# Radial weights ahead of the second transposed block in the first edge pass of a graph kernel

## The chip, the cores and the metric

One core of a Trainium2 chip runs the whole program. The metric is the device time of one execution in microseconds. The chip has a matrix engine (TensorE, PE in the rows), a vector engine (VectorE, DVE), an activation engine (ScalarE, ACT), a general engine that here only issues gathers (GpSimd, POOL) and an engine that issues DMAs (SyncE, SP). Each works through its own instructions in order; they meet at semaphores.

## The reference

Two message-passing layers over a graph with 12,500 nodes and 200,000 edges, each with a residual and a layer norm. The change concerns the edges of the first layer. For each edge, with `y0, y1` from `edge_attr_4` and weights `w1` from `edge_attr_16`:

```python
msg_s = (s_n @ Ws_src)[src] + (s_n @ Ws_dst)[dst]          # 64 scalars
msg_v = (v_n x Wv_src)[src] + (v_n x Wv_dst)[dst]          # 32 vectors of 3
w1 = rbf @ W_rbf                                           # radial weights, 224 an edge
m1_s, m1_v = _cg_tp(msg_s, msg_v, y0, y1, *parts of w1)    # first product
a = leaky(m1_s @ W_alpha) . alpha_dot                      # logits of 4 heads
val_s = m1_s @ Ws_val;  val_v = (m1_v x Wv_val) * sigmoid(val_s @ Wg)
m2_s, m2_v = _cg_tp(sigmoid(val_s), val_v, y0, y1, w2...)  # second product
h = concat(m2_s @ Ws_vlin, m2_v x Wv_vlin)                 # values of 4 heads
```

A softmax over each node's edges, the weighted sum, a projection and the second layer follow in later passes.

## The kernel before

The kernel runs its passes one after the other; the first edge pass is the function `edges`. It takes the edges in 392 groups of 512, a group being 4 tiles of 128 edges. An edge is a partition (row) for VectorE's products; TensorE needs channels in the partitions, so each product is transposed by TensorE into PSUM (`ps_t`, two banks in turn), and ScalarE copies each bank out (`take`), after which TensorE multiplies by weights.

The order of work is written out by hand, an instruction list for each engine in a `body(u, ...)` that a loop repeats four groups at a time (`rounds`). Everything waits on counting semaphores: `first` counts VectorE's steps of the first product (14 a group), `turned` TensorE's blocks, `taken` ScalarE's copies, `radial` and `weighted` the radial weights made and scaled, `second`, `third`, `mixed`, `gated`, `headed`, `kept`, `valued` later steps. The loops are staggered: while group u has its first product transposed, the radial weights of u + 1 are made, the second product of u - 1 is under way, and the values of u - 2.

Steps that matter here, with their names in the profile:
- VectorE: `message` adds the two gathered rows (e_msg). `products_with_y` multiplies them by scaled harmonics that stand beside the radial weights in PSUM (e_vy and e_c, L1013), so it waits for `weighted`. Sums and cross products follow, then `heads_with_y` (e_partial), `scalars_by_weights`, `heads_sum` (e_h, L1014), `vectors_by_weights` and `cross_by_weights`; with the last of these `first` reaches 14. In one group of four `leaky` (logits) follows and waits for ScalarE's `keep`. The next group's messages alternate with the gating of the group before.
- TensorE: `radial_weights(u + 1)` is four bf16 matmuls (L784) into `ps_w`, a single buffer: it waits until VectorE has finished group u. `scalars`, `vectors`, `last_block` are four transposes each (L793), of the first, second and third block of the first product. `vectors` waits for the same count of `first` as `radial_weights`. `first_layer` (L809) waits for the second `take`; `values(u - 2)` (L849, L850), `mix(u)` (L818 to L820, waits for the third `take`), `second_blocks(u - 1)` (L793) and `heads(u - 1)` (L838, waits for VectorE's e_h) follow in this order.
- ScalarE: `harmonics` issues the DMA that loads `y` of group u + 1 (L916), `store` one of results; then three times `take` (L886), `with_y0` (L963 once and L966 four times: copies the harmonics beside the radial weights and scales the weights by y0 in place; waits for `radial` and the load of `y`), the hidden layer (L901, L902), `second_with_y0` (L941), the gate and logits (L905 to L907, waits for `mixed`), two takes of the second product (e_m2t), and `keep` (e_above L926, e_partial L928, waits for `headed`).
- GpSimd issues the gathers three groups ahead; SyncE loads indices and radial bases.

Of the kernel before, what the change touches and what calls it, by code (L numbers as in the profile page):

```python
# [35 lines left out]
RING = 4  # L36
# [32 lines left out]
def wait(engine, sem, value):  # L69

    if not isinstance(value, int) or value > 0:
        engine.wait_ge(sem, value)
# [466 lines left out]
def edges(nc, walk, idx_d, y_d, rbf_d, table_src, table_dst, h_d, w, ident, logits, issued, dst_windows, dst_i, windows_in):  # L539
# [13 lines left out]
    with ExitStack() as ctx:  # L553
# [99 lines left out]
        def turn(u, second_tp, k):  # L653


            if second_tp:
                return u * 6 + ((5 if isinstance(u, int) and u == groups - 1 else 9) + k)
            return k + 1 if isinstance(u, int) and u == 0 else u * 6 + (k - 1)
# [13 lines left out]
        def present(u):  # L672

            return not isinstance(u, int) or 0 <= u < groups
# [94 lines left out]
        def _(pe):  # L769
# [10 lines left out]
            def radial_weights(u, r, i):  # L780
                pe.wait_ge(rbf_in[r], (i + 1) * 16 * len(PARTS_OF_PAIRS))
                wait(pe, first, u * FIRST)
                for t in range(T):
                    last = nc.tensor.matmul(radial_w[:, t, 0:WN],  # L784
                                            rbf[:, r, t * P:(t + 1) * P], stack_rbf[:], start=True, stop=True)
                last.then_inc(radial, 1)

            def turn_block(place, bank, rows):

                wait(pe, taken, place - 2)  # L790
                for t in range(T):
                    channels = rows(t).shape[1]
                    last = nc.tensor.transpose(ps_t[bank][0:channels, t * P:(t + 1) * P], rows(t), ident[:])  # L793
                last.then_inc(turned, 1)

            def scalars(u):
                pe.wait_ge(first, u * FIRST + DONE_S)
                turn_block(turn(u, False, 0), 0, lambda t: m1[:, t, 0:MID])

            def vectors(u):  # L800
                pe.wait_ge(first, (u + 1) * FIRST)
                turn_block(turn(u, False, 1), 1, lambda t: m1[:, t, MID:MID + P])

            def last_block(u):
                turn_block(turn(u, False, 2), 0, lambda t: m1[:, t, MID + P:MID + 2 * P])

            def first_layer(u):
                pe.wait_ge(taken, turn(u, False, 1))
                nc.tensor.matmul(ps_t[1][:], w_first[:], m1t[0:MID, 0, :], start=True, stop=True).then_inc(turned, 1)  # L809
# [43 lines left out]

            def body(u, r, i):
                scalars(u)
                vectors(u)
                if present(u + 1):
                    radial_weights(u + 1, (r + 1) % RING, i + (r + 1) // RING)
                last_block(u)
                first_layer(u)  # L860
                values(u - 2)
                mix(u)
                second_blocks(u - 1)
                heads(u - 1, (r - 1) % 2)

            radial_weights(0, 0, 0)
            rounds(pe, body)
            values(groups - 2)
            second_blocks(groups - 1)
# [3 lines left out]
        @block.scalar  # L873
        def _(act):
            act.wait_ge(ones_set, 1)

            def rotations(r):

                vector = y[:, r, :, 1:4]
                lanes, tiles, components = vector.ap  # L880
                return bass.AP(vector.tensor, vector.offset, [lanes, tiles, [components[0], 3], components])

            def take(place, bank, into):
                act.wait_ge(turned, place)
                rows = into.shape[0]
                nc.scalar.activation(into, ps_t[bank][0:rows, :], ACT.Copy).then_inc(taken, 1)  # L886

            def body(u, r, i):
                slot = r % 2
                wait(act, mixed, u)  # L890
                if present(u + 1):
                    harmonics(u + 1, (r + 1) % RING)
                store(u - 3, 1 - slot)
                take(turn(u, False, 0), 0, m1t[0:MID, 0, :])
                take(turn(u, False, 1), 1, m1t[:, 1, :])
                take(turn(u, False, 2), 0, m1t[:, 2, :])
                with_y0(u + 1, (r + 1) % RING, i + (r + 1) // RING)
                act.wait_ge(turned, turn(u, False, 3))
                wait(act, headed, u - 1)

                nc.scalar.activation(hidden[0:CS, slot, :], ps_t[1][0:CS, :], ACT.Relu, scale=0.8)  # L901
                nc.scalar.activation(hidden[CS:P, slot, :], ps_t[1][CS:P, :], ACT.Sigmoid).then_inc(taken, 1)  # L902
                second_with_y0(u - 1, (r - 1) % RING)
                act.wait_ge(mixed, u + 1)
                nc.scalar.activation(gate, gate, ACT.Sigmoid)  # L905
                nc.scalar.activation(second_y, rotations(r), ACT.Copy)
                nc.scalar.activation(logits[:, bass.ds(u * T, T), :], mix_v[:, :, LIN:LIN + HEADS],  # L907
                                     ACT.Copy).then_inc(gated, 1)
                take_second(u - 1)
                keep(u - 1, (r - 1) % RING, 1 - slot, i)  # L910

            def harmonics(u, r):

                if present(u - RING):
                    act.wait_ge(third, (u - RING + 1) * THIRD)
                act.dma_start(y[:, r], y_d[u]).then_inc(y_in[r], 16)  # L916

            def keep(v, r, slot, i):
                if not present(v):
                    return  # L920
                act.wait_ge(headed, v + 1)
                if present(v - 2):
                    act.wait_ge(third, (v - 1) * THIRD)
                if r == 0:
                    wait(act, leaked, i)
                nc.scalar.activation(above[:, r], mix_h[:, :, HL:HL + HEADS], ACT.Copy)  # L926
                for t in range(T):
                    last = nc.scalar.activation(partial[:, slot, t, HS:HA], mix_h[:, t, HS:HA], ACT.Copy,  # L928
                                                scale=y[:, r, t, 0:1])
                last.then_inc(kept, 1)  # L930

            def second_with_y0(v, r):

                if not present(v):
                    return
                act.wait_ge(second, v * SECOND + GV)
                if present(v - 1):
                    act.wait_ge(turned, turn(v - 1, True, 1))
                for t in range(T):
                    into = m2[:, t, 0:6 * CV].rearrange("p (x k c) -> p x k c", x=3, k=2)  # L940
                    last = nc.scalar.activation(into[:, :, 0, :], gv[:, t], ACT.Copy, scale=y[:, r, t, 0:1])  # L941
                last.then_inc(scaled_v, 1)

            def take_second(v):
                if not present(v):
                    return
                wait(act, valued, v)
                take(turn(v, True, 0), 0, m2t[:, 0, :])
                take(turn(v, True, 1), 1, m2t[0:MID, 1, :])

            def store(v, slot):
                if not present(v):
                    return
                act.wait_ge(third, (v + 1) * THIRD)
                act.dma_start(h_d[v], h_rows[:, slot].rearrange("p t k -> p (t k)")).then_inc(stored[slot], 16)

            def with_y0(u, r, i):

                if not present(u):
                    return  # L960
                act.wait_ge(radial, u + 1)
                act.wait_ge(y_in[r], (i + 1) * 16)
                nc.scalar.activation(first_y, rotations(r), ACT.Copy)  # L963
                for t in range(T):
                    of_tile = radial_w[:, t, W_SS:W_SS + MID]
                    last = nc.scalar.activation(of_tile, of_tile, ACT.Copy, scale=y[:, r, t, 0:1])  # L966
                last.then_inc(weighted, 1)

            harmonics(0, 0)
            with_y0(0, 0, 0)  # L970
            rounds(act, body)
            second_with_y0(groups - 1, RING - 1)
            take_second(groups - 1)
            store(groups - 3, (groups - 3) % 2)
            keep(groups - 1, RING - 1, (groups - 1) % 2, 0)
            store(groups - 2, groups % 2)
            store(groups - 1, (groups - 1) % 2)
            for slot in range(2):
                act.wait_ge(stored[slot], 16 * (groups // 2))
# [1573 lines left out]
```

## Time and profile before

| | us |
|---|---|
| median of 3 runs | 9161.6 |
| lowest, highest | 9114.37, 9190.41 |
| the profiled execution | 9135.79 |
| its span in the profile | 9134.0 |
| first radial matmul of the pass, start | 242.9 |
| last radial matmul of the pass, start | 5470.6 |

The profile shows one execution. Its span runs from the first to the last instruction; the execution's own time is 1.8 us longer. The first edge pass fills the span from about 243 to about 5,500 us. Ends of matmuls are modelled, not observed. In the timeline, instructions of one kind in a row are merged (x4), with the time from the start of the first to the end of the last, and the bracket at the end is the time that the engine was idle before and what ended it.

### The profile page before, as it was taken

What the parts mean: (1) busy time and instruction counts of PE and PEld (TensorE: products, weight loads), DVE (VectorE), ACT (ScalarE), POOL (GpSimd) and SP (SyncE); (2) the same over time, 40 slices, a digit from 0 to 9 for tenths busy, and PEclk for the clock granted to TensorE, in tenths of its full rate; (3) what the DMA queues carried; (4) which work ended last, traced back from release to release, by engine and by line L of the source; (5) the groups of instructions that cost most, each with busy time, mean ns of one, the idle gap of its engine ahead of it and who ended that gap; (6) DMA issues with size and microseconds to landing.
All of it is one profiled execution on the core that took longest, in us unless ns stands there. A gap on an engine that the chain in (4) does not pass through costs nothing. (4 is left out here: it accounts for less than half of the span.)

```text
span 9134.0 us, 197714 instructions
## 1 busy us (share of the span) xinstructions
PE 7569.2 (83%) x43972; PEld 5972.6 (65%) x43973; DVE 6766.6 (74%) x16742; ACT 5161.1 (57%) x16950; POOL 5109.3 (56%) x5222
## 2 busy tenths in 40 slices
PE   5788888888888888888888886997778888888788
PEld 3677777777777777777777776995444444444446
DVE  7777777777777777777777787887667767767677
ACT  5555555555555555555555552116666666667675
POOL 0556666555555555655655555870666655566650
PEclk7788888888788788888888797998899989999999
DMA  7333333223222232322332234766444434444345
GB/s 251 79 83 87 85 85 84 79 83 85 79 83 83 79 85 83 84 83 81 84 83 83 82 80 150 236 204 112 107 110 111 112 106 110 111 109 114 108 110 180
DMA packets 971877, 968.06 MB, mean 106 GB/s; under 512 B 452750, under 2 KB 788750, under 8 KB 971662
## 3 DMA queue, kind: packets, MB, share of 16 engines
q0 software_dynamic: 225792, 385.65, 17.1%
q1 hardware_dynamic: 512032, 346.40, 13.8%
q10 hardware_dynamic: 233936, 234.90, 7.7%
q14 instruction: 98, 0.80, 0.0%
q8 instruction: 19, 0.31, 0.0%
HBM read 677.57 MB, written 288.65 MB: 106 GB/s over the span
## 5 line engine op out<-in xcount | busy, mean ns | idle before, releaser
L754 POOL DMA_INDIRECT e_g_dst<-table_dst,e_idx x1568 | 1518.9, 969 | 1159.5 <-issue 622.8
L754 POOL DMA_INDIRECT e_g_src<-table_src,e_idx x1568 | 1560.9, 995 | 996.6 <-issue 803.3
L2028 POOL DMA_INDIRECT f_e<-table,f_src x1568 | 1494.0, 953 | 980.1 <-issue 530.3
L793 PE MATMUL e_ps_t<-ident,e_m 128*128 128x128 f32 (+1 forms) x7840 | 1405.9, 331 | 471.1 <-issue 193.2
L793 PEld LDWEIGHTS e_ps_t<-ident,e_m 128*128 128x128 f32 (+1 forms) x7840 | 1121.6, 168 | 618.4 <-issue 365.8
L2085 PE MATMUL f_ps_a<-sums 128*128 128x384 f32 x3936 | 1524.3, 534 | 1.5 <-DVE sums L2185 1.5
L2085 PEld LDWEIGHTS f_ps_a<-sums 128*128 128x128 f32 x3936 | 767.6, 205 | 576.0 <-issue 228.7
L886 ACT ACTIVATE e_m1t<-e_ps_t 128x512 f32<-128x512 f32 (+1 forms) x1176 | 669.1, 597 | 548.9 <-PE e_ps_t L809 198.1
L2074 PE MATMUL f_ps_w<-f_w,f_hidden 64*128 64x192 f32 x3936 | 495.1, 374 | 470.3 <-DVE sums L2185 232.3
L1013 DVE TENSOR_TENSOR e_vy<-e_msg,e_ps_w 128x384 f32<-128x384 f32 x392 | 216.5, 552 | 839.5 <-issue 522.1
L905 ACT ACTIVATE e_ps_v<-e_ps_v 128x128 f32<-128x128 f32 x392 | 102.7, 262 | 1252.7 <-remote 733.3
L838 PE MATMUL e_ps_h<-e_w_hs,e_hidden 128*128 128x100 f32 x3136 | 582.1, 345 | 257.3 <-DVE e_h L1014 195.4
L838 PEld LDWEIGHTS e_ps_h<-e_w_hs,e_hidden 128*128 128x128 f32 x3136 | 516.1, 249 | 357.7 <-DVE e_h L1014 281.9
L849 PEld LDWEIGHTS e_ps_h<-e_w_h,e_m2t 128*128 128x128 f32 x3136 | 562.7, 211 | 229.1 <-issue 217.6
L819 PE MATMUL e_ps_v<-e_w_v,e_m1t 128*128 128x64 f32 x3136 | 709.4, 311 | 1.5 <-issue 1.4
L850 PE MATMUL e_ps_h<-e_w_h,e_m2t 96*128 96x96 f32 x3136 | 705.1, 310 | 0.0
L2074 PEld LDWEIGHTS f_ps_w<-f_w,f_hidden 64*128 64x128 f32 x3936 | 337.1, 201 | 554.7 <-DVE sums L2185 279.1
L2185 DVE TENSOR_TENSOR f_ey<-f_e,f_ps_w 128x384 f32<-128x384 f32 x492 | 272.5, 554 | 558.6 <-ACT f_ps_w L2118 264.3
L820 PE MATMUL e_ps_v<-e_w_v,e_m1t 128*128 128x64 f32 x3136 | 666.4, 297 | 2.5 <-DVE e_m L1015 1.2
L2130 ACT ACTIVATE sums<-iota,f_rel 128x128 f32<-128x128 f32 x1968 | 628.6, 390 | 16.0
L818 PE MATMUL e_ps_v<-e_w_gate,e_m1t 96*128 96x36 f32 x3136 | 615.1, 282 | 24.8 <-DVE e_d L1013 11.8
L849 PE MATMUL e_ps_h<-e_w_h,e_m2t 128*128 128x64 f32 x3136 | 598.7, 275 | 2.4 <-ACT e_partial L928 2.4
(268 smaller groups left out, 17539.2 us busy)
## 6 DMA issues: line engine op xcount, KB each, us to landing
edge_values<-e_h ACTq DMA_DIRECT2D x392, 330.0 KB
r_h<-edge_values SPq DMA_DIRECT2D x196, 660.0 KB, 4.0
sums<-sums ACTq DMA_DIRECT2D x492, 192.0 KB
e_g_src<-table_src,e_idx POOLq DMA_INDIRECT x1568
e_g_dst<-table_dst,e_idx POOLq DMA_INDIRECT x1568
f_e<-table,f_src POOLq DMA_INDIRECT x1568
f_rbf<-basis SPq DMA_DIRECT2D x492, 48.0 KB
basis<-t_part SPq DMA_DIRECT2D x42, 448.0 KB, 3.1
```

Source lines behind the costliest of these rows:

```text
L754: pool.indirect_dma_start(out=into[:, r, t, :], out_offset=None, in_=table, in_offset=bass.IndirectOffsetOnAxis(ap=idx[:, r, c:c + 1], axi ...
L793: last = nc.tensor.transpose(ps_t[bank][0:channels, t * P:(t + 1) * P], rows(t), ident[:])
L819: nc.tensor.matmul(mix_v[:, t, VS:VS + 2 * CV], m1t[:, 1, tile], w_v1[:], start=True, stop=True)
L820: last = nc.tensor.matmul(mix_v[:, t, VS + 2 * CV:VS + 4 * CV], m1t[:, 2, tile], w_v2[:], start=True, stop=True)
L838: last = nc.tensor.matmul(mix_h[:, t, HS:HL + HEADS], hidden[:, slot, t * P:(t + 1) * P], w_hs[:], start=True, stop=True)
L849: nc.tensor.matmul(mix_h[:, t, 0:2 * CV], m2t[:, 0, tile], w_h1[:], start=True, stop=True)
L850: last = nc.tensor.matmul(mix_h[:, t, 2 * CV:HA], m2t[0:MID, 1, tile], w_h2[:], start=True, stop=True)
L886: nc.scalar.activation(into, ps_t[bank][0:rows, :], ACT.Copy).then_inc(taken, 1)
L2028: pool.indirect_dma_start(out=rows_of_units[:, (place * RING + r) * T + t, :], out_offset=None, in_=table, in_offset=bass.IndirectOffsetOn ...
L2074: last = nc.tensor.matmul(ps_w[r % 2][:, t * 256:t * 256 + WE], hidden[rows, r % 2, n * P:(n + 1) * P], w_2[rows, :], start=True, stop=True)
L2085: last = nc.tensor.matmul(ps_a[slot][:, 0:ACC1], onehot[:, r, t, :], q[:, r, t, :], start=t == 0, stop=t == T - 1)
L2130: last = nc.scalar.activation(apart[:, r % 2, t, :], iota[:], ACT.Abs, bias=rel[:, r % 2, t:t + 1])
```

## The change

TensorE's list makes the radial weights of group u + 1 after the first block of transposes, ahead of the second one. ScalarE's list scales them after the first `take`, ahead of the second and third one. Nothing else differs: the instructions, buffers, tiles and other waits are the same.

```diff
--- before.py
+++ after.py
@@ -853,9 +853,9 @@
 
             def body(u, r, i):
                 scalars(u)
-                vectors(u)
                 if present(u + 1):
                     radial_weights(u + 1, (r + 1) % RING, i + (r + 1) // RING)
+                vectors(u)
                 last_block(u)
                 first_layer(u)
                 values(u - 2)
@@ -892,9 +892,9 @@
                     harmonics(u + 1, (r + 1) % RING)
                 store(u - 3, 1 - slot)
                 take(turn(u, False, 0), 0, m1t[0:MID, 0, :])
+                with_y0(u + 1, (r + 1) % RING, i + (r + 1) // RING)
                 take(turn(u, False, 1), 1, m1t[:, 1, :])
                 take(turn(u, False, 2), 0, m1t[:, 2, :])
-                with_y0(u + 1, (r + 1) % RING, i + (r + 1) // RING)
                 act.wait_ge(turned, turn(u, False, 3))
                 wait(act, headed, u - 1)
```

## Rows read from the trace of the kernel before

**Rows 1.** Page, part 1: busy time, share of the span and instructions of each engine.

```profile
PE 7569.2 (83%) x43972; PEld 5972.6 (65%) x43973; DVE 6766.6 (74%) x16742; ACT 5161.1 (57%) x16950; POOL 5109.3 (56%) x5222
```

**Rows 2.** Busy time by engine in 500:5400, then granted clock, DMA share, GB/s.

```profile
500.00:5400.00 4900.00, 4169.29 (x26992) 3668.71 (x26991) 3672.54 (x9216) 2718.94 (x8753) 2884.76 (x2939) 0.83 0.31 83
```

**Rows 3.** Groups by line, 500:5400: count | busy, mean ns | idle before, releasers.

```profile
L838 PE MATMUL e_ps_h<-e_w_hs,e_hidden 128*128 128x100 f32 x2913 | 540.1, 344 | 241.2 <-DVE e_h L1014 180.9 <-issue 53.3
...
L809 PE MATMUL e_ps_t<-e_m1t,e_w_first 96*128 96x512 f32 x730 | 462.3, 719 | 28.0 <-ACT e_m1t L886 15.1 <-issue 12.6
...
L784 PE MATMUL e_ps_w<-e_stack_rbf,e_rbf 96*128 96x224 bf16 x1457 | 248.7, 303 | 0.0
...
L1013 DVE TENSOR_TENSOR e_vy<-e_msg,e_ps_w 128x384 f32<-128x384 f32 x365 | 201.6, 552 | 799.3 <-issue 498.5 <-ACT e_ps_w L966 300.8
...
L905 ACT ACTIVATE e_ps_v<-e_ps_v 128x128 f32<-128x128 f32 x365 | 95.6, 262 | 1189.2 <-remote 706.4 <-PE e_ps_v L820 443.9 <-issue 38.6
...
L926 ACT ACTIVATE e_above<-e_ps_h 128x16 f32<-128x16 f32 x364 | 67.1, 184 | 287.2 <-PE e_ps_h L838 230.4 <-issue 29.8 <-remote 26.8
...
L1014 DVE TENSOR_TENSOR logits<-logits,e_above 128x64 f32 x91 | 20.6, 226 | 241.2 <-ACT e_partial L928 153.1 <-issue 88.1
```

**Rows 4.** Timeline, ScalarE, one group: start, duration, instruction, idle before.

```profile
3195.07 0.18 ACT L926 ACTIVATE e_above<-e_ps_h 128x16 f32<-128x16 f32 x1 [1.07 <-PE e_ps_h L838]
...
3195.29 0.34 ACTq L916 DMA_DIRECT2D e_y<-harmonics  x1
...
3196.27 1.08 ACT L886 ACTIVATE e_m1t<-e_ps_t 96x512 f32<-96x512 f32 x2 [0.19 <-PE e_ps_t L793]
3198.69 0.60 ACT L886 ACTIVATE e_m1t<-e_ps_t 128x512 f32<-128x512 f32 x1 [1.34 <-PE e_ps_t L809]
3199.18 0.20 ACT L963 ACTIVATE e_ps_w<-e_y 128x36 f32<-128x36 f32 x1
3199.30 1.00 ACT L966 ACTIVATE e_ps_w<-e_ps_w,e_y 128x96 f32<-128x96 f32 x4
...
3205.87 0.26 ACT L905 ACTIVATE e_ps_v<-e_ps_v 128x128 f32<-128x128 f32 x1 [3.27 <-remote]
...
3206.23 1.07 ACT L886 ACTIVATE e_m2t<-e_ps_t 128x512 f32<-128x512 f32 x2
3207.84 0.18 ACT L926 ACTIVATE e_above<-e_ps_h 128x16 f32<-128x16 f32 x1 [0.54 <-PE e_ps_h L838]
```

**Rows 5.** Timeline of VectorE, the same group.

```profile
3200.43 0.56 DVE L1013 TENSOR_TENSOR e_vy<-e_msg,e_ps_w 128x384 f32<-128x384 f32 x1 [4.60 <-issue]
...
3203.65 0.55 DVE L1013 TENSOR_TENSOR e_partial<-e_ps_h,e_y 128x384 f32<-128x384 f32 x1
...
3204.91 0.81 DVE L1014 TENSOR_TENSOR e_h<-e_partial,e_ps_h 128x640 f32<-128x640 f32 x1
```

**Rows 6.** Timeline of TensorE, the same group.

```profile
3194.83 1.21 PE L793 MATMUL e_ps_t<-ident,e_m 128*96 128x128 f32 x8
3195.88 0.55 PE L784 MATMUL e_ps_w<-e_stack_rbf,e_rbf 96*128 96x224 bf16 x4
3196.92 0.66 PE L793 MATMUL e_ps_t<-ident,e_m 128*128 128x128 f32 x4 [0.49 <-issue]
3197.41 1.12 PE L809 MATMUL e_ps_t<-e_m1t,e_w_first 96*128 96x512 f32 x2
...
3199.87 0.41 PE L850 MATMUL e_ps_h<-e_w_h,e_m2t 96*128 96x96 f32 x2
...
3202.55 0.39 PE L820 MATMUL e_ps_v<-e_w_v,e_m1t 128*128 128x64 f32 x2
...
3205.77 2.03 PE L838 MATMUL e_ps_h<-e_w_hs,e_hidden 128*128 128x100 f32 x8 [1.02 <-issue]
```

**Rows 7.** DMA issues of the whole run: count, KB, us to landing.

```profile
t_wb<-w_Wv_src SPq DMA_DIRECT2D x4, 4.0 KB, 1.7
...
m_wp_b<-w_Wpv SPq DMA_DIRECT2D x4, 4.0 KB, 4.9
```

## The prediction

> **What bounds the kernel now.** I began with the page's busy shares: TensorE 83%, VectorE 74%, ScalarE 57% of the span [rows 1], so no engine is full and the change must be judged by waits. The edited stage is the first edge pass. The window 500:5400 lies inside it, with TensorE busy 4169.29 of 4900 us and VectorE 3672.54, at a granted clock of 0.83 [rows 2]. Grouping by line in that window gives 365 groups (one "e_vy<-e_msg" each) [rows 3], so a group of 512 edges takes 4900/365 = 13.42 us, and the pass has 392 of them.
>
> Next I asked the same rows for the idle time ahead of each instruction. VectorE loses nearly all it loses in one place: 799.3 us, 2.19 us a group, ahead of the first product with the scaled radial weights, ended mostly by "issue" and by ScalarE's L966, the instruction that scales them [rows 3]. That is what the change aims at. But three other waits recur too: TensorE 241.2 us ahead of the heads matmuls (0.66 a group, mostly for VectorE's e_h), ScalarE 287.2 us ahead of e_above (0.79 a group, for those matmuls), and ScalarE 1189.2 us ahead of the gate (3.26 a group) [rows 3].
>
> Then I walked one typical group (12.77 us from one e_above to the next) on the three engines. ScalarE: e_above 3195.07; the first two takes 3196.27 to 3197.35; the third 3198.69; radial scaling 3199.18 to 3200.30; the gate only at 3205.87; the second product's takes until 3207.30; next e_above 3207.84 [rows 4]. VectorE: first product 3200.43, e_h 3204.91 to 3205.72 [rows 5]. TensorE: first and second transposes 3194.83 to 3196.04, radial weights 3195.88, third transposes 3196.92, first layer 3197.41, last of the mixing matmuls 3202.55, heads 3205.77 to 3207.80 [rows 6]. So there are **two loops through the same e_above**:
> - Loop A: first take, (second and third take), radial scaling, VectorE's products to e_h, heads, e_above. It closes the group here: heads start 0.05 us after e_h ends.
> - Loop B: first and second take, first layer, value and mixing matmuls, gate, two takes of the second product, e_above. Here it ends at 3207.30, only 0.54 us ahead of loop A.
> The reader is to see how close they are: A is shortened by the change and B is lengthened.
>
> **The change part by part.** No instruction is added or removed. On TensorE four radial matmuls pass four transposes; on ScalarE five activations pass two takes. Both waits that move along are met: the radial matmuls wait for the same count of VectorE as the second transposes did, and TensorE was idle 0.0 us ahead of the radial matmuls in the window, so their inputs were always there [rows 3].
>
> 1. *Radial weights earlier.* They took 3195.88 to 3196.43 and now start where the second transposes did, halfway through the eight at about 3195.43, so they are done by about 3196.0, ahead of the end of the first take at 3196.27 + 0.60 = 3196.87 (0.60 as the third one took) [rows 4, 6]. No cost. The second transposes come 0.55 us later, end by 3196.6 instead of about 3196.05, and their take is not ready to begin before 3197.9 now, so that is covered too. If TensorE's signals come late (below), the cover is gone and ScalarE's whole queue waits behind the scaling; bounds 0 and about 1 us.
>
> 2. *Scaling earlier.* It starts at about 3196.8 instead of 3199.18, 2.4 us earlier; VectorE can use 2.19 a group on average, its idle time. Not all: in one group of four VectorE waits 241.2/91 = 2.65 us for ScalarE's e_partial ahead of the logits sum [rows 3], and this wait stands ahead of its messages and gating, which come before the next product, so in these groups the product gains nothing. What the group gains is bounded by what waits for VectorE at the other end: 0.66 us (TensorE ahead of heads) to 0.79 us (ScalarE ahead of e_above). In the group walked, loop B takes over after 0.54. I take a gain of 0.5; bounds 0 and 0.79.
>
> 3. *The harmonics' transfer.* The scaling reads what ScalarE's queue issued at 3195.29 [rows 4]. That was 3.9 us before its use, now 1.5. Its landing isn't shown; the nearest rows are 4 KB loads at 1.7 us and, farther, 4.9 us in a busier stage [rows 7]. So 0.1 to 3.4 us of wait; I take 0.1, by the row of 1.7 us.
> The Trainium skill (DMA: Bandwidth & Descriptors, Anatomy of one DMA) gives a fixed cost of about 2.0 us whatever the size; by it the wait would be 0.5 us, 0.4 more a group and some 150 us in all. The 1.7 us row here is under that figure.
>
> 4. *Second and third take later.* The scaling lasts 1.12 us (3199.18 to 3200.30) and now lies ahead of the second take, which ends at about 3198.45 instead of 3197.35. Queued behind it are the third take and, on TensorE, the first layer, which waits for the second take; behind that in TensorE's order are the value matmuls, the mixing, the second transposes and the heads. First layer: 3197.41 becomes 3198.5, +1.1 us. The granted clock of 0.83 on average [rows 2] says that TensorE spends a third of the time at the lower of its two levels (1.2 against 2.4 GHz); there its transposes last longer and the first layer comes later anyway, so the mean is less; bounds 0.4 and 1.1, I take 1.0. The third take is not delayed: it waited for TensorE until 3198.69 and now ends near 3199.05.
>
> 5. *How much of that 1.0 us reaches the gate.* The last mixing matmul is shown ending at 3202.94, yet ScalarE's gate, with nothing else to wait for, starts at 3205.87 [rows 4, 6]; over all groups such waits, ended by "remote", make 706.4/365 = 1.94 us [rows 3]. TensorE's signals are up to 3 us behind its shown ends. If this is backlog that a pause works off, a pause of 1 us ahead of the first layer costs less than 1 us; if it is a delay after each burst, the pause costs all of itself. No row tells which; bounds 0 and 1.0 given back, I take 0.4.
> The Trainium skill (Perfetto Trace Analysis, Tensor Engine Instruction) says that the profiler estimates a matmul's end and that the semaphore follows only after PSUM's acknowledgement. The trace agrees that the shown end is no signal, with 2.93 us between the two here.
>
> Per group: -0.5 (step 2) + 0.1 (step 3) + 1.0 (step 4) - 0.4 (step 5) = +0.2 us. Times 392: +78 us. The profiled execution took 9135.8 us (span 9134.0), 26 under the median of the three runs (9161.6) and inside their range. 9135.8 + 78 = 9214, rounded to **9215 us**.
>
> **The rivals.**
> - *Loop A's gain comes through*: the pause is absorbed in the late signals. For it: VectorE's 2.19 us a group, and heads released by e_h within 0.05 us. Against: only 0.66 to 0.79 us can come back. Net -0.3 to -0.5 a group: 9018 to 8940 us.
> - *Loop B takes the place of A at its full new length* (the other side): the second take stands behind the scaling, the first layer starts 1.0 us later, and the delay reaches the gate whole. It decides as soon as more than the 0.5 us of slack arrives. Net -0.4 + 1.0 + 0.1 = +0.7: 9410 us. For it: loop B was 0.54 us behind, and TensorE at 4169.29 of 4900 has little to catch up with. At the lower clock level its work is longer and its slack smaller still.
> - *VectorE's gain stops halfway*: after the cross products it reads the value matmuls' result. It read it at 3203.65 [rows 5] and would come at about 3201.3, while these matmuls, shown ending at 3200.28 before [rows 6], now end at 3201.4 plus the late signal. It then waits 0.1 to 3 us of the 2.4. e_h is still earlier than now in most groups, so this costs nothing alone; it takes step 2 towards 0. With that: +0.7 as above.
>
> **How the numbers follow.** About 1%, some 92 us or 0.23 us a group, is what the measurement can tell from no change. Forecast case (within 0.23 of zero either way, likeliest value +0.2): 0.38. Loop A's gain: 0.27, faster by over 1%. Loop B in full, with its variants between +0.23 and +0.8: 0.35, slower by over 1%. The range takes most of the first rival (-0.32 x 392 = -125) and most of the second (+0.68 x 392 = +265): 9010 to 9400 us.
>
> **What the changed profile would show.** VectorE's idle time ahead of "e_vy<-e_msg" under 0.8 us a group (right for steps 1 and 2); TensorE's wait for e_h ahead of heads nearly gone; a new wait ahead of the first layer (L809) of about 1 us a group for ScalarE's takes (step 4); VectorE waiting ahead of "e_partial<-e_ps_h" for the value matmuls. A wait of the scaling for harmonics over 0.3 us would prove step 3 wrong. Step 5 shows in the "remote" idle time ahead of the gate: below 1.94 us a group means that the pause is absorbed. The prediction fails towards faster if that falls by 1 us, towards slower if it stays.

## The result, and the profile after

| | us |
|---|---|
| before, median of 3 runs | 9161.6 (9114.37 to 9190.41) |
| changed, median of 3 runs | 9564.66 (9563.63 to 9600.56) |
| ratio | 1.046, 95% interval 1.042 to 1.0501 |
| changed, the profiled execution | 9600.56 (span 9598.8) |

The changed kernel is 4.6% slower, 403 us by the medians. Nearly all of the loss is in the first edge pass: its last radial matmul starts at 5921.8 us, against 5470.7 before, which is 451 of the 465 us by which the two spans differ.

The page, parts 1 and 2 (the second line is the granted clock of TensorE in 40 slices of the span, in tenths). TensorE is busy for 288 us more than before with the same 43972 instructions [rows 1]: the work has become longer, not more.

```profile
PE 7856.8 (82%) x43972; PEld 6286.7 (65%) x43973; DVE 6785.1 (71%) x16742; ACT 5214.9 (54%) x16950; POOL 5131.4 (53%) x5222
...
PEclk7777777778778787888887887899899999999999
```

Two more lines of the kernel before, in the window 500:5400: count | busy, mean ns of one | idle before, with releasers.

```profile
L819 PE MATMUL e_ps_v<-e_w_v,e_m1t 128*128 128x64 f32 x2920 | 662.1, 312 | 1.5 <-issue 1.4
...
L1013 DVE TENSOR_TENSOR e_partial<-e_ps_h,e_y 128x384 f32<-128x384 f32 x365 | 200.1, 548 | 44.4 <-remote 31.8 <-PE e_ps_h L850 10.8 <-issue 1.2
```

The changed kernel in the same window:

```profile
L819 PE MATMUL e_ps_v<-e_w_v,e_m1t 128*128 128x64 f32 x2688 | 704.7, 353 | 0.0
...
L809 PE MATMUL e_ps_t<-e_m1t,e_w_first 96*128 96x512 f32 x672 | 462.7, 776 | 423.0 <-ACT e_m1t L886 230.4 <-issue 192.4
L838 PE MATMUL e_ps_h<-e_w_hs,e_hidden 128*128 128x100 f32 x2683 | 459.1, 329 | 36.5 <-DVE e_h L1014 28.3 <-issue 7.9
...
L1013 DVE TENSOR_TENSOR e_partial<-e_ps_h,e_y 128x384 f32<-128x384 f32 x336 | 186.6, 555 | 324.6 <-PE e_ps_h L850 230.6 <-issue 58.7 <-remote 31.4
...
L1013 DVE TENSOR_TENSOR e_vy<-e_msg,e_ps_w 128x384 f32<-128x384 f32 x336 | 184.6, 549 | 417.0 <-issue 285.9 <-ACT e_ps_w L966 130.6
...
L905 ACT ACTIVATE e_ps_v<-e_ps_v 128x128 f32<-128x128 f32 x335 | 87.8, 262 | 1400.1 <-PE e_ps_v L820 1130.4 <-remote 222.2 <-issue 47.4
L963 ACT ACTIVATE e_ps_w<-e_y 128x36 f32<-128x36 f32 x336 | 69.8, 208 | 107.0 <-DMA e_y<-harmonics 47.0 <-remote 27.5 <-issue 24.9
...
L926 ACT ACTIVATE e_above<-e_ps_h 128x16 f32<-128x16 f32 x336 | 62.0, 185 | 205.4 <-PE e_ps_h L838 187.7 <-remote 17.2 <-issue 0.6
```

And the busy time of the window by engine (TensorE, its weight loads, VectorE, ScalarE, GpSimd), then granted clock, DMA share, GB/s.

```profile
500.00:5400.00 4900.00, 4072.55 (x24859) 3635.48 (x24857) 3394.41 (x8483) 2551.43 (x8061) 2659.30 (x2693) 0.79 0.28 76
```

There are 336 groups in 4900 us, so a group takes 14.58 us instead of 13.42. Against [rows 3], per group:
- VectorE waits 417.0/336 = 1.24 us ahead of e_vy (before 2.19) and now also 324.6/336 = 0.97 us ahead of e_partial, for the value matmuls (before 44.4/365 = 0.12).
- TensorE waits 36.5/336 = 0.11 us for e_h ahead of the heads (before 0.66). Loop A has let go.
- TensorE waits 423.0/336 = 1.26 us ahead of the first layer, for ScalarE's takes (before 28.0/365 = 0.08). This is the new wait.
- ScalarE's "remote" idle time ahead of the gate is 222.2/335 = 0.66 us (before 1.94).
- ScalarE waits 107.0/336 = 0.32 us ahead of the scaling, of which 47.0/336 = 0.14 us for the load of the harmonics.
- The same mixing matmul (L819) takes 353 ns on average, before 312. This is what the prediction has no term for. The granted clock of the window is 0.79, before 0.83 [rows 2].

Two groups of the changed kernel, only one group between them, show what a mean hides. Stretches by window, same columns; the first is a whole group, the second another whole group, the third and fourth two parts that make up nearly all of that second one.

```profile
3716.10:3727.69 11.59, 9.59 (x76) 8.38 (x75) 10.37 (x28) 7.61 (x24) 6.91 (x7) 1.00 0.32 89
...
3739.80:3757.47 17.67, 14.51 (x66) 13.09 (x65) 10.59 (x28) 7.75 (x24) 9.18 (x10) 0.61 0.24 68
3739.80:3743.40 3.60, 0.77 (x6) 0.42 (x4) 1.47 (x4) 2.96 (x12) 2.62 (x3) 1.00 0.61 176
3743.40:3757.20 13.80, 13.47 (x58) 12.40 (x59) 8.85 (x24) 4.78 (x13) 6.29 (x8) 0.51 0.14 37
```

One group lasts 11.59 us at a clock of 1.00, the other 17.67 us. In the first 3.6 us of the long one TensorE is busy for 0.77 us, at full clock still; then the granted clock falls to the lower level, and the 13.8 us behind it hold 13.47 us of matmuls. TensorE's timeline in the short group (start, duration, instruction, idle before):

```profile
3717.94 0.66 PE L793 MATMUL e_ps_t<-ident,e_m 128*128 128x128 f32 x4 [0.50 <-issue]
3719.89 1.12 PE L809 MATMUL e_ps_t<-e_m1t,e_w_first 96*128 96x512 f32 x2 [1.29 <-ACT e_m1t L886]
...
3722.61 0.34 PE L818 MATMUL e_ps_v<-e_w_gate,e_m1t 96*128 96x36 f32 x2
...
3724.79 0.41 PE L819 MATMUL e_ps_v<-e_w_v,e_m1t 128*128 128x64 f32 x2
...
3725.26 1.04 PE L793 MATMUL e_ps_t<-ident,e_m 128*128 128x128 f32 x8
```

and in the long one:

```profile
3741.67 0.66 PE L793 MATMUL e_ps_t<-ident,e_m 128*128 128x128 f32 x4 [1.76 <-issue]
3743.73 2.08 PE L809 MATMUL e_ps_t<-e_m1t,e_w_first 96*128 96x512 f32 x2 [1.40 <-issue]
...
3748.96 0.53 PE L818 MATMUL e_ps_v<-e_w_gate,e_m1t 96*128 96x36 f32 x2
...
3753.14 0.67 PE L819 MATMUL e_ps_v<-e_w_v,e_m1t 128*128 128x64 f32 x2
...
3754.02 1.92 PE L793 MATMUL e_ps_t<-ident,e_m 128*128 128x128 f32 x8
```

TensorE idles for 1.76 us ahead of the third transposes (0.50 in the short group). They are over at 3742.33, the first layer starts at 3743.73 after another 1.40 us without a matmul, and then lasts 2.08 us instead of 1.12; the mixing takes 5.3 us (3748.96 to 3754.23) instead of 2.8 (3722.61 to 3725.4). ScalarE's timeline in the long group tells why TensorE paused: the scaling lies between the first take and the two others, and the gate then waits out the slow matmuls.

```profile
3741.03 0.59 ACT L886 ACTIVATE e_m1t<-e_ps_t 96x512 f32<-96x512 f32 x1 [0.22 <-issue]
...
3742.17 0.99 ACT L966 ACTIVATE e_ps_w<-e_ps_w,e_y 128x96 f32<-128x96 f32 x4
3743.06 1.10 ACT L886 ACTIVATE e_m1t<-e_ps_t 128x512 f32<-128x512 f32 x2
...
3754.27 0.26 ACT L905 ACTIVATE e_ps_v<-e_ps_v 128x128 f32<-128x128 f32 x1 [6.04 <-PE e_ps_v L820]
```

I took groups 20 to 379 from the records of both kernels, from one e_above to the next, and sorted them by the share of each that fell under the lower level (1.2 GHz) of the granted clock:

| share at the low level | before: groups, mean us | after: groups, mean us |
|---|---|---|
| under 1% | 66, 12.36 | 142, 12.41 |
| 1% to 65% | 245, 13.03 | 98, 13.69 |
| over 65% | 49, 16.84 | 120, 17.67 |
| all | 360, 13.43 | 360, 14.51 |

**At the high level the change costs and brings nothing; most of the loss is in where the low level falls.** From the start of the first layer to the gate, a group spent 1.97 us at the low level before and 4.03 us after; in the rest of the group that time fell from 2.57 to 1.93 us. A straight line, fitted in each kernel to the lengths of the groups with these two times, starts at 12.32 us in both. With the low-level times of before, the line of the changed kernel gives 13.61 us, so by this estimate some 0.9 of the added 1.1 us come from the low level's new place and 0.2 from the rest. As a mean over the groups, 16% of the stretch of the mixing and 15% of that of the values lay at the low level before, 43% and 40% after; for the first block of transposes it fell from 46% to 24%. Before, TensorE's long pause lay ahead of the heads, and the heads and the short transposes behind it bore much of the slow stretch; now a longer one lies ahead of its longest unbroken work.

The Trainium skill (TensorE: Matmul & The Clock Gate, A second HAM failure mode: psum-queue depth-cycling) tells of another kernel that short, frequent idle times of TensorE between groups of matmuls made its clock swing between the two levels. The traces here agree that it swings, with a mean grant of 0.83 before and of 0.79 with 1.26 us of pause a group ahead of the first layer.

### The profile page after: what moved, and what is told of

Read it like the earlier page. It is cut to its first block and busy times, and to the rows that moved or that the text cites. A ratio compares the mean times of both kernels' runs of the same rounds, so it can differ in the third digit from the quotient of the medians.

```text
span 9598.8 us, 197330 instructions
## 1 busy us (share of the span) xinstructions
PE 7856.8 (82%) x43972; PEld 6286.7 (65%) x43973; DVE 6785.1 (71%) x16742; ACT 5214.9 (54%) x16950; POOL 5131.4 (53%) x5222
## 5 line engine op out<-in xcount | busy, mean ns | idle before, releaser
L793 PE MATMUL e_ps_t<-ident,e_m 128*128 128x128 f32 (+1 forms) x7840 | 1364.0, 315 | 417.5 <-issue 211.6
L793 PEld LDWEIGHTS e_ps_t<-ident,e_m 128*128 128x128 f32 (+1 forms) x7840 | 1064.0, 162 | 545.0 <-issue 279.5
L809 PE MATMUL e_ps_t<-e_m1t,e_w_first 96*128 96x512 f32 x784 | 537.8, 774 | 489.5 <-ACT e_m1t L886 256.2
L819 PE MATMUL e_ps_v<-e_w_v,e_m1t 128*128 128x64 f32 x3136 | 821.3, 353 | 0.0
L850 PE MATMUL e_ps_h<-e_w_h,e_m2t 96*128 96x96 f32 x3136 | 817.8, 351 | 0.0
L849 PEld LDWEIGHTS e_ps_h<-e_w_h,e_m2t 128*128 128x128 f32 x3136 | 652.8, 244 | 248.1 <-issue 210.8
L820 PE MATMUL e_ps_v<-e_w_v,e_m1t 128*128 128x64 f32 x3136 | 774.5, 338 | 0.0
L818 PE MATMUL e_ps_v<-e_w_gate,e_m1t 96*128 96x36 f32 x3136 | 706.6, 315 | 0.3 <-issue 0.3
L849 PE MATMUL e_ps_h<-e_w_h,e_m2t 128*128 128x64 f32 x3136 | 681.7, 307 | 2.4 <-ACT e_partial L928 2.4
L818 PEld LDWEIGHTS e_ps_v<-e_w_gate,e_m1t 96*128 96x128 f32 x3136 | 640.5, 253 | 1.6 <-issue 1.6
L820 PEld LDWEIGHTS e_ps_v<-e_w_v,e_m1t 128*128 128x128 f32 x3136 | 640.8, 253 | 0.0
L819 PEld LDWEIGHTS e_ps_v<-e_w_v,e_m1t 128*128 128x128 f32 x3136 | 640.4, 252 | 0.0
```

Of the source, the lines that this page charges most:

```text
L818: nc.tensor.matmul(mix_v[:, t, 0:VS], m1t[0:MID, 0, tile], w_gate[:], start=True, stop=True)
L819: nc.tensor.matmul(mix_v[:, t, VS:VS + 2 * CV], m1t[:, 1, tile], w_v1[:], start=True, stop=True)
L820: last = nc.tensor.matmul(mix_v[:, t, VS + 2 * CV:VS + 4 * CV], m1t[:, 2, tile], w_v2[:], start=True, stop=True)
L849: nc.tensor.matmul(mix_h[:, t, 0:2 * CV], m2t[:, 0, tile], w_h1[:], start=True, stop=True)
L850: last = nc.tensor.matmul(mix_h[:, t, 2 * CV:HA], m2t[0:MID, 1, tile], w_h2[:], start=True, stop=True)
```

## The experiments

Ratios are each kernel's to the kernel before, measured beside it on the same chip. The kernel before took 9094.88 us beside e1 to e4 (chip 2), 9486.02 beside e5 to e8 and 9495.25 beside e9 to e12 (both chip 4), and 9085.69 beside e13 to e15 (chip 0). So times are compared on one chip only, and waits or mean durations of e5 to e12 stand beside those of a kernel before whose profiled execution took 9135.79 us.

**Theories.** *Queue*: the first layer's delay passes through to the gate. *Clock*: the pause ahead of the first layer brings the lower clock to the value and mixing matmuls. *Earlier VectorE work* (contention) and *TensorE's order* are further rivals.

**e1, the delay alone.** On the kernel before:

```diff
             def first_layer(u):
-                pe.wait_ge(taken, turn(u, False, 1))
+                pe.wait_ge(taken, turn(u, False, 2))
```

> The kernel before, with one wait changed: the first layer waits for ScalarE's third take instead of the second. Nothing of VectorE's work comes earlier, so this is the delay of the first layer alone. Before, the first layer starts about 2.7 us after e_above and the third take ends about 4.1 us after it, so the delay is some 1.4 us a group. If a delay there passes whole to the end of the group (theory of the queue), +0.9 to 1.3 us a group of 392, 9,500 to 9,650 us. If a delay alone is absorbed and only TensorE's clock costs (theory of the clock), the groups at the high clock level keep their length (12.4 to 12.9 us) and more groups run at the low one. If both are absorbed: under 9,250 us.

Measured 9750.53 us, ratio 1.0705 (1.0648 to 1.0762). Groups by line, 500:5400:

```profile
L819 PE MATMUL e_ps_v<-e_w_v,e_m1t 128*128 128x64 f32 x2616 | 713.1, 366 | 0.0
...
L809 PE MATMUL e_ps_t<-e_m1t,e_w_first 96*128 96x512 f32 x656 | 436.1, 751 | 463.7 <-ACT e_m1t L886 286.3 <-issue 177.4
```

The pause is 463.7/328 = 1.41 us a group and L819 takes 366 ns. By the records of groups 20 to 379 the first layer starts 1.3 us later than before. The groups with under 1% at the low level lasted 12.46 us, against 12.36 before; 112 instead of 49 had over 65%, and the low level took 4.66 us a group between first layer and gate, against 1.97. So a delayed first layer without any of the change's other effects makes more than the whole loss. Where the clock holds, the delay is absorbed; where it doesn't, it is not: these groups last 17.70 us, against 16.84.

**e2, e13, e14, e15, the pause filled with useless work.** On the changed kernel; e15 issues these transposes twice:

```diff
+            def fill(u):
+                for t in range(T):
+                    nc.tensor.transpose(ps_t[0][:, t * P:(t + 1) * P], m1[:, t, MID + P:MID + 2 * P], ident[:])
...
                 vectors(u)
+                pe.wait_ge(taken, turn(u, False, 0))
+                fill(u)
                 last_block(u)
```

> The changed kernel, with the third block's transposes made twice: four more transposes a group, in the stretch in which TensorE would only wait for the second take. The first layer still waits for that take, so the delay stays and only the pause is filled. Theory of the clock (the pause lets the granted clock fall for the value and mixing matmuls): fewer groups at the low level, about 9,200 to 9,400 us. Theory of the queue (the first layer's delay is passed on): as the changed kernel, 9,565 us, or up to 100 us more for the added work.

> The changed kernel again, unaltered, so that it and the filled ones stand against the same runs of the kernel before on one chip. Ratio 1.04 to 1.05, as in its own result.

> e2 again (four more transposes in the wait for the second take) on the chip of e13. Theory of the clock: 0.015 to 0.03 in the ratio under e13. If e2's lower ratio came from another chip, the two are equal, or this one is above e13.

> Eight more transposes a group instead of four, 1.1 us or more of work without use. The pause left in e2 ahead of the first layer (0.7 us a group) falls to about 0.3. Theory of the clock: the value and mixing matmuls run at the high level as often as in the kernel before or more (mean of L819's counterpart under 320 ns), ratio 1.00 to 1.025, limited by the added work where the clock is low. Theory of the queue: the ratio rises over e13's by the added work.

| | added | us | ratio | interval |
|---|---|---|---|---|
| e2 | 4 transposes | 9286.89 | 1.0224 | 1.0165 to 1.0283 |
| e13 | none | 9562.63 | 1.0535 | 1.0473 to 1.0596 |
| e14 | 4 transposes | 9266.31 | 1.0169 | 1.0097 to 1.0241 |
| e15 | 8 transposes | 9126.5 | 1.0032 | 1.0007 to 1.0057 |

Groups by line and the window, e13, e14 (L823 and L813 are its L819 and L809) and e15:

```profile
L819 PE MATMUL e_ps_v<-e_w_v,e_m1t 128*128 128x64 f32 x2672 | 706.0, 356 | 0.0
...
L809 PE MATMUL e_ps_t<-e_m1t,e_w_first 96*128 96x512 f32 x668 | 454.7, 768 | 438.0 <-ACT e_m1t L886 251.9 <-issue 185.7
```

```profile
500.00:5400.00 4900.00, 4068.36 (x24726) 3640.19 (x24725) 3377.37 (x8434) 2534.06 (x8017) 2643.51 (x2673) 0.79 0.29 76
```

```profile
L823 PE MATMUL e_ps_v<-e_w_v,e_m1t 128*128 128x64 f32 x2832 | 668.2, 323 | 0.0
...
L813 PE MATMUL e_ps_t<-e_m1t,e_w_first 96*128 96x512 f32 x709 | 472.3, 753 | 264.7 <-issue 154.8 <-ACT e_m1t L892 109.4
```

```profile
500.00:5400.00 4900.00, 4112.49 (x27620) 3653.53 (x27618) 3577.20 (x8946) 2671.47 (x8502) 2824.16 (x2842) 0.86 0.30 80
```

```profile
L823 PE MATMUL e_ps_v<-e_w_v,e_m1t 128*128 128x64 f32 x2912 | 652.4, 309 | 0.0
...
L813 PE MATMUL e_ps_t<-e_m1t,e_w_first 96*128 96x512 f32 x726 | 436.6, 685 | 113.2 <-issue 66.4 <-ACT e_m1t L892 44.4
```

```profile
500.00:5400.00 4900.00, 4197.03 (x29807) 3751.06 (x29807) 3668.88 (x9173) 2719.43 (x8717) 2905.77 (x2926) 0.90 0.31 83
```

The pause goes from 438.0/334 = 1.31 us a group to 0.75 to 0.31; the mixing matmul from 356 ns to 323 to 309; the granted clock from 0.79 to 0.86 to 0.90. The changed kernel gets **436 us faster by eight transposes a group that nobody reads**. By the theory of the queue it had to get slower, so that theory alone can't hold. By the records of groups 20 to 379 the first layer starts 3.81 us after e_above in e2 and in e15 and 3.80 in the changed kernel, so its lateness alone is not the price; the time at the low level between first layer and gate is 2.20 us a group in e2 and 1.28 in e15, against 4.03.

**e7, the same amount of work in the wrong place.** The last tile's three mixing matmuls are issued twice, in the changed kernel:

```diff
-                for t in range(T):
+                for t in (*range(T), T - 1):
                     tile = slice(t * P, (t + 1) * P)
                     nc.tensor.matmul(mix_v[:, t, 0:VS], ...
```

> Control for the filled pause: the changed kernel with as much added work (the last tile's three mixing matmuls issued twice, about 0.7 us a group), but in the dense stretch and not in the pause. Theory that the filled pause helped since it was filled: no gain here, 0.7 us x 392 = 270 us more, ratio 1.06 to 1.08. Theory that any added TensorE work holds the clock up: a ratio under 1.04.

Measured 10097.92 us, ratio 1.0643 (1.061 to 1.0676). The changed kernel wasn't measured on that chip, but e5, whose pause is the same and which loses as much, was at 1.0454. More work in this dense stretch costs; the same amount in the pause helped.

**e5 and e6, the halves of the change.** e5 moves only the scaling on ScalarE, e6 only the radial matmuls on TensorE; each is one hunk of the diff.

> Only ScalarE's half of the change: the scaling ahead of the second and third take, TensorE's order as before. The first layer waits for the second take behind the scaling just as in the changed kernel, and the radial weights come 0.6 us later. If the pause ahead of the first layer is the cause, the loss is the changed kernel's or larger: ratio to the kernel before 1.04 to 1.06.

> Only TensorE's half of the change: radial weights between the first and second transposes, ScalarE's order as before. The second take comes some 0.5 us later at most and no pause opens ahead of the first layer. Expected: within 1% of the kernel before (ratio 0.995 to 1.01). A ratio over 1.03 would say that TensorE's order, not ScalarE's, made the loss.

e5: 9900.8 us, 1.0454 (1.0424 to 1.0484), pause 425.5/327 = 1.30 us. e6: 9625.54 us, 1.0179 (1.0124 to 1.0234), pause 157.9/341 = 0.46 us, L819 328 ns. ScalarE's half alone makes a loss as large as the whole one. I had expected e6 within 1%. The second take ends 0.6 us later there, by the moved transposes, and opens a smaller pause; but the scaling, still behind all three takes, starts later too (4.30 us after e_above, before 3.97), and VectorE waits 906.8/341 = 2.66 us for it (before 2.19):

```profile
L1013 DVE TENSOR_TENSOR e_vy<-e_msg,e_ps_w 128x384 f32<-128x384 f32 x341 | 188.8, 554 | 906.8 <-ACT e_ps_w L966 481.3 <-issue 425.5
```

How e6's loss divides between the two is not shown.

**e3 and e12, useful work in the pause.**

```diff
                 last_block(u)
-                first_layer(u)
                 values(u - 2)
+                first_layer(u)
                 mix(u)
```

e3 does this to the changed kernel, e12 to the kernel before.

> The changed kernel, with the value matmuls of group u - 2 ahead of the first layer instead of behind it: 2 us of useful work fill the pause, and the mixing matmuls start about 1 us earlier than in the changed kernel. Both theories expect a gain over 9,565 us here. If the late first layer was all of the loss and loop A's gain is real, the time falls to 9,000 to 9,150 us, under the kernel before. If the hidden layer, now later by 2 us, holds ScalarE and the second product up, it stays at 9,300 us or above.

> The kernel before with the value matmuls ahead of the first layer and nothing else. It has hardly a pause ahead of the first layer (0.08 us a group), so the theory of the pause expects no gain: ratio 0.99 to 1.01. A ratio near 0.98 would say that e3's return to the level of before came from the value matmuls' place itself, not from the filled pause.

e3: 9111.29 us, 1.0001 (0.9975 to 1.0026). e12: 9519.91 us, 1.0045 (1.0017 to 1.0073). Groups by line of e3:

```profile
L819 PE MATMUL e_ps_v<-e_w_v,e_m1t 128*128 128x64 f32 x2912 | 686.5, 322 | 0.2 <-issue 0.2
...
L809 PE MATMUL e_ps_t<-e_m1t,e_w_first 96*128 96x512 f32 x728 | 441.6, 692 | 37.5 <-ACT e_m1t L886 19.6 <-issue 17.1
```

The pause is 0.10 us, L819 is back at 322 ns, and the loss is gone; e12 shows that the new place of the value matmuls brings nothing by itself. But I had hoped for less than the time before, and that isn't there, though ScalarE's wait ahead of the gate is down to 610.1/365 = 1.67 us and VectorE's ahead of e_vy to 396.8/364 = 1.09. What bounds e3 was not tried.

**e4, e9, e10, the scaling between the second and third take.** ScalarE's order is take, take, scaling, take. e9 leaves TensorE's order as before, e4 takes the changed one, e10 the changed one with the value matmuls first.

> TensorE's order as changed; ScalarE scales the radial weights between the second and the third take instead of between the first and the second. The first layer isn't delayed, the third take is (by 1.1 us, and the mixing matmuls reach it later than that). Scaling starts about 1.7 us earlier than before. Theory that the second take's delay behind the scaling is the cause of the loss: the loss is gone, and a part of the gain shows, 8,950 to 9,150 us. Theory that earlier VectorE work itself is the cause (contention, a lower clock from a denser TensorE): slower than before, 9,250 us or more.

> TensorE's order as before; ScalarE scales the radial weights between the second and the third take. Compared with the run e4, the second transposes are not moved behind the radial matmuls, so the second take isn't later and the first layer keeps its place: idle time ahead of it under 0.15 us a group (e4 had 0.26, the kernel before 0.08). Theory of the pause ahead of the first layer: no loss, ratio 0.985 to 1.00. Were e4's loss due to earlier VectorE work, it would stay: 1.01.

> e4 (scaling between second and third take, radial weights between first and second transposes) with the value matmuls ahead of the first layer. No pause ahead of the first layer in any case. Theory: ratio 0.98 to 1.00, at least 0.01 under e4's 1.012.

e4: 9202.79 us, 1.0116 (1.0065 to 1.0167), pause 92.8/358 = 0.26 us. e9: 9453.9 us, 0.9955 (0.992 to 0.9989). e10: 9492.62 us, 0.9969 (0.9948 to 0.9991). Groups by line of e9:

```profile
L838 PE MATMUL e_ps_h<-e_w_hs,e_hidden 128*128 128x100 f32 x2832 | 496.0, 330 | 158.6 <-DVE e_h L1014 95.9 <-issue 60.8
L809 PE MATMUL e_ps_t<-e_m1t,e_w_first 96*128 96x512 f32 x708 | 480.4, 767 | 34.0 <-issue 20.6 <-ACT e_m1t L886 12.8
...
L1013 DVE TENSOR_TENSOR e_vy<-e_msg,e_ps_w 128x384 f32<-128x384 f32 x354 | 195.0, 551 | 443.2 <-issue 255.1 <-ACT e_ps_w L966 188.1
```

e9 takes 0.94 us off VectorE's wait ahead of e_vy (443.2/354 = 1.25 us), keeps the pause at 34.0/354 = 0.10 us, and is 0.45% faster than the kernel before, a small gain with 1 just outside its interval. e4 was expected at or under the time before and is over it. It has TensorE's changed order and 0.26 us of pause, but they were not separated, and VectorE's wait for e_vy is 514.4/358 = 1.44 us there, so that the pause makes e4's loss is argued, not shown. e3 and e9 speak against earlier VectorE work as a cause of the loss: the scaling starts 2.10 us after e_above in e3, as early as in the changed kernel, and neither loses.

**e8 and e11, other small pauses.** The radial matmuls are issued twice, where TensorE waits for the first take: e8 in the kernel before, e11 in e3.

> The kernel before, with the four radial matmuls issued twice (some 0.55 us a group at the high clock level), which lies in the stretch where TensorE waits about 0.5 us for the first take ahead of the third block. Theory of the clock: this small pause matters too, fewer matmuls at the low level, ratio 0.98 to 1.00. Theory that only the pause of over 1 us matters: ratio 1.00 to 1.02.

> e3 (the changed kernel with the value matmuls ahead of the first layer) and the radial matmuls issued twice, 0.55 us a group of work without use where TensorE waits for the first take. e3 was at a ratio of 1.000. If pauses anywhere in the group let the clock fall, 0.98 to 1.00; if only the one ahead of the first layer does, 1.00 to 1.02.

e8: 9500.59 us, 1.0005 (0.9981 to 1.003). e11: 9502.68 us, 0.9984 (0.9952 to 1.0015). Doubling 0.55 us of work a group (over 200 us in all) costs nothing and brings nothing. These two don't separate the theories: the pause there is only 0.5 us, and transposes stand behind it.

## Why the prediction was wrong, point by point

- *What bounds the kernel*: two loops through e_above, 0.54 us apart. Right in kind, though VectorE's 799.3 us ahead of e_vy were not nearly all that it lost: it was idle for 1227 of the 4900 us, 241.2 of them ahead of the logits sum. The heads' wait for e_h fell from 0.66 to 0.11 us, and loop B took over.
- *Step 1, radial weights in time*: right. The scaling starts about 2.1 us after e_above, by the records of groups 20 to 379, where it was 4.0.
- *Step 2, gain of 0.5 us*: right in kind. VectorE's wait fell by 0.95 us, not to under 0.8; e_partial waits 0.97 us for the value matmuls, as the third rival said, and the second product's first step (e_mixed_v) 1.05 us for ScalarE's gate (before 0.34).
- *Step 3, 0.1 us for the harmonics*: right. ScalarE is idle for 0.32 us a group ahead of the scaling, and 0.14 us of it ends with this load's landing. The wait of 0.5 us by the Trainium skill's figure did not come; the section named in the prediction (DMA: Bandwidth & Descriptors, Anatomy of one DMA) is on DMAs that GpSimd issues, and this one is ScalarE's.
- *Step 4, first layer 1.0 us later*: right, 2.69 to 3.80 us after e_above, +1.1 us. The third take does come later too, by 0.3 us (4.08 to 4.38).
- *Step 5, how much of it reaches the gate*: **the step that failed.** I bounded the price of a pause between nothing and its own length, with every matmul as long as in the profile of before. The missing term is the clock: from first layer to gate, the time at the low level went from 1.97 to 4.03 us a group, some 0.9 us of price by the estimate above. The value and mixing matmuls, from the start of the former to the end of the latter, went from 5.3 to 6.2 us a group on average.

From one e_above to the next the records give, per group: first layer later +1.11, its own length +0.10, values and mixing longer +0.96, signal behind the shown end -0.96, from the gate to the next e_above -0.12, together +1.09 us (13.43 to 14.51). The forecast was +0.2, with +1.0, nothing, nothing, -0.4 and -0.4 (steps 2 and 3 together) in these places. Read alone, these means mislead: they look as if late signals had paid for the slower matmuls and the delay had passed whole. The groups that stay at one level tell it apart (us, means):

| | first layer after e_above | from there to the gate | of it, signal behind the shown end | gate to next e_above | group |
|---|---|---|---|---|---|
| under 1% low, before | 2.43 | 7.01 | 1.38 | 2.92 | 12.36 |
| under 1% low, after | 3.51 | 6.74 | 1.20 | 2.17 | 12.41 |
| over 65% low, before | 3.41 | 10.21 | 0.04 | 3.22 | 16.84 |
| over 65% low, after | 4.10 | 10.31 | 0.04 | 3.27 | 17.67 |

At the high level the delay of 1.08 us is given back: 0.75 behind the gate, which is step 2's slack, and 0.27 ahead of it, of which 0.18 in the signals (step 5 took 0.4). At the low level the signal comes 0.04 us behind the shown end, nothing is left to give back, and the delay of 0.69 us passes on. The rest of the loss is that far more groups are of the slow kind. Much of the fall of the signals' delay on average, and of "remote" by 1.28 us, is these groups.

- *The rivals*: the second one had the direction and the place, and its 9410 us fell short by the same term. It said that the delay reaches the gate whole through the queue. That happens in the groups at the low level, of which it also said that their slack is smaller; at the high level it doesn't, and e1, e14 and e15 show that the price goes with the clock. I had read the mean grant of 0.83 and used it only to make step 4 smaller.
- *The range*: 9400 was its end, 9564.66 the result. No bound stood for a longer matmul.

Not settled is what decides in which groups the clock falls: the long group above had idled for 1.76 and 1.40 us ahead of its third transposes and first layer, the short one for 0.50 and 1.29, and no run separated the two pauses. Nor is it settled in full why e15, with the highest clock of all (0.90), isn't faster than before. By its records the groups with under 1% at the low level last 12.80 us, against 12.36 before, so its added work costs some 0.4 us where the clock holds; the third take ends 5.88 us after e_above there instead of 4.08, which was not tried apart.

## What to carry to other kernels

Before a reorder opens a new idle time of TensorE, look at what stands behind it: with a pause of 1.26 us ahead of the longest unbroken run of matmuls a group took 1.16 us more here, although the groups that kept the full clock took only 0.05 us more. What the pause of 0.66 us ahead of heads and short transposes had cost before, no run shows. An instruction that shortens one wait may be placed one step later (after the copy that TensorE waits for) and shorten that wait without the pause: e9 did, with 0.94 us less of it a group, and gained 0.45%. If the page of the profile shows a mean clock under 1.00, durations are not constants of the sum: price the matmuls at both levels.

## What the runs showed of the hardware that I had not expected

Useless transposes in TensorE's idle time made the program 4.6% faster (9562.63 to 9126.5 us) by a granted clock of 0.90 instead of 0.79. The same kernel before took 9085.69 us on one chip and 9495.25 on another, at a median granted clock of 0.866 and 0.844 over the whole run, with ratios of variants nonetheless near each other (1.0535 for the changed kernel on the first, 1.0454 for its ScalarE half on the second). And where values and mixing ran at full clock in the kernel before, ScalarE's wait for them ended between 0.04 and 7 us after the last matmul's shown end (median 2 us, over 4 us in one group of ten), while at the low level it ended with it: 0.04 us in the median of 49 groups and 0.22 at most, as at 3754.27 for a matmul shown ending at 3754.23.
